# Expert outputs with w3 stationary on two column halves, and the mixing moved from VectorE to TensorE

## What is computed

```python
logits = x @ gate_w + gate_b
top_probs, top_idx = top_k(softmax(logits), 2)          # two experts of 16 for each token
dispatch = sum(one_hot(top_idx) * top_probs / sum(top_probs))
hidden = silu(x @ w1[e]) * (x @ w2[e])                  # for every expert e: 64 -> 128
expert_out = hidden @ w3[e]                             # 128 -> 64
out = h + sum_e expert_out[e] * dispatch[:, e]
```

## Time and profile before

| | us |
|---|---|
| median of 3 runs | 2246.7 |
| lowest and highest | 2244.17 and 2251.53 |
| profiled execution, own time | 2242.19 |
| its span | 2240.4 |

### The profile page before, as it was taken

One profiled execution on the slowest core, in us unless ns is written; L12 is line 12 of the kernel. 1 busy time (PEld: TensorE's weight loads), 2 busy tenths in 40 slices (PEclk: granted clock), 3 DMA queues, 4 the chain that ended last, 5 costly groups with the idle time before them and its releaser, 6 DMA issues.

```text
span 2240.4 us, 45957 instructions
## 1 busy us (share of the span) xinstructions
PE 2017.2 (90%) x15249; PEld 1837.6 (82%) x15249; DVE 1996.7 (89%) x6209; ACT 942.2 (42%) x2040; POOL 1454.0 (65%) x1657
## 2 busy tenths in 40 slices
PE   2468999989898999999899998989999998999899
PEld 1356789889798988889798897989888898988788
DVE  1257899999999999999999999999999999999998
ACT  1224443444444444444444444444444444433333
POOL 0388767578585858758575775858587685858700
PEclk9779999999999999999999999999999999998999
DMA  8787536466564646666463665746376674532200
GB/s 200 214 238 207 172 106 179 139 186 194 162 189 112 182 123 193 188 169 194 111 183 111 189 191 165 198 114 188 104 197 183 169 199 120 175 88 85 68 3 6
DMA packets 363145, 346.80 MB, mean 155 GB/s; under 512 B 49312, under 2 KB 313632, under 8 KB 362784
## 3 DMA queue, kind: packets, MB, share of 16 engines
q1 hardware_dynamic: 313760, 209.59, 34.8%
q0 software_dynamic: 49152, 134.28, 20.1%
HBM read 205.89 MB, written 137.89 MB: 153 GB/s over the span
## 4 chain that ended last, share of the span: by engine, by line
PE 60%; DVE 27%; issue 8%; POOL 2%; DMA 1%; ACT 1%; DVEq 0%; POOLq 0%; ACTq 0%
PE bank_o L637 15%; PE bank_h L628 10%; PE bank_h L629 9%; PE bank_d L693 9%; PE bank_d L703 7%; DVE ob L975 5%; DVE hid L964 4%; DVE wsam L1053 2%; DVE v_sb L1088 2%; PE bank_a L715 2%; PE bank_p L658 2%; POOL gath L574 2%; DVE v_sb L1081 2%; PE bank_p L657 1%; PE bank_p L663 1%
## 5 line engine op out<-in xcount | busy, mean ns | idle before, releaser
L574 POOL DMA_INDIRECT gath<-table,idx x1024 | 1127.0, 1101 | 271.4 <-issue 237.5
L637 PEld LDWEIGHTS bank_o<-w_sb,hid 128*128 128x128 f32 x4608 | 636.2, 199 | 75.4 <-issue 60.6
L637 PE MATMUL bank_o<-w_sb,hid 128*128 128x64 f32 x4608 | 630.8, 275 | 43.7 <-DVE ob L975 42.6
L628 PE MATMUL bank_h<-xsplit,w 128*128 128x384 f32 x1536 | 616.4, 401 | 28.3 <-DVE hid L964 27.7
L787 ACT ACTIVATE silu<-bank_h 128x384 f32<-128x384 f32 x768 | 380.6, 496 | 481.5 <-PE bank_h L629 476.5
L629 PE MATMUL bank_h<-xsplit,w 128*128 128x384 f32 x1536 | 532.0, 346 | 0.0
L975 DVE SCALAR_TENSOR_TENSOR ob<-bank_o,disp,ob 128x64 f32<-128x64 f32 x2160 | 474.5, 276 | 3.7 <-PE bank_o L637 3.4
L964 DVE TENSOR_TENSOR hid<-silu,bank_h 128x384 f32<-128x384 f32 x768 | 420.6, 548 | 25.1 <-ACT silu L787 18.2
L628 PEld LDWEIGHTS bank_h<-xsplit,w 128*128 128x128 f32 x1536 | 301.2, 196 | 59.4 <-DVE hid L964 35.2
L1053 DVE TENSOR_TENSOR wsam<-gath,cw 128x1024 f32<-128x1024 f32 x256 | 312.3, 1220 | 25.8 <-DMA gath<-table,idx 19.6
L693 PE MATMUL bank_d<-eye,wsam 128*128 128x128 f32 x2048 | 281.8, 283 | 30.1 <-DVE wsam L1053 26.6
(11 more groups left out here) (142 smaller groups left out, 1864.4 us busy)
## 6 DMA issues: line engine op xcount, KB each, us to landing
table<-pixmaj SPq DMA_DIRECT2D x80, 1024.0 KB, 10.0
xin<-x_dram SPq DMA_DIRECT2D x256, 256.0 KB
table<-pixmaj SPq DMA_DIRECT2D x32, 960.0 KB
table<-pixmaj SPq DMA_DIRECT2D x16, 1088.0 KB
gath<-table,idx POOLq DMA_INDIRECT x1024
out_dram<-ob SPq DMA_DIRECT2D x48, 96.0 KB
gath<-w_dram SPq DMA_DIRECT2D x4, 512.0 KB, 9.3
interp_sb<-interp_dram SPq DMA_DIRECT2D x1, 1024.0 KB, 5.5
```

Of the source, the lines that this page charges most:

```text
L574: pool.indirect_dma_start(out=gath[buf][:, p, :, :].rearrange("p a c -> p (a c)"), out_offset=None, in_=table[par], in_offset=bass.Indirec ...
L628: mm(bank[:, 0:GC], w12[:, e, which, 0, :], xsplit[gp][:], start=True, stop=False)
L637: last = mm(bank_o[n % 2][:, C * k:C * (k + 1)], hid[:, n % HB, 128 * k:128 * (k + 1)], w3_sb[:, e, :], start=True, stop=True)
```

## The change

W is done for a pair of experts q = 0 to 7 of a group, with w3 stationary (64 columns) and `hid` moving (384 columns): the first expert of the pair writes partitions 0 to 63 of the one bank `bank_o`, the second partitions 64 to 127. So the outputs have channels on the partitions and tokens on the columns, and the dispatch weight is no longer a scalar of the partition. The new steps:

- P9: PE transposes the dispatch weights of a group (3 transposes of 64 columns) into `bank_p`, ACT copies them to `dispT`. P8 gets two more small DVE instructions, which split the weights into a rounded and a remaining part.
- R, for each pair: one float32r matmul of 384 columns with the 128 x 128 matrix `sel` spreads the two weight rows of the pair over 64 partitions each, into `bank_p`; ACT copies them to `wide[q]`. R of pair q waits for the copy of q - 1, as there is one bank.
- W on DVE, for each pair: `scaled` = `bank_o` x `wide[q]` (384 columns, a ring of 5). W on PE waits for the product of the pair before.
- Z, for each half group: PE transposes 4 `scaled` blocks for each of 3 token blocks, accumulating in `bank_z` (12 transposes of 128 x 128).
- M2, for each half group: DVE adds both halves of `bank_z` to `ob` (2 instructions of 192 columns).
- O: SP stores the group (was M2). The setup gets three DVE instructions more and one small load.

X, its `hid` and all other steps are as before. The wait of `hid` for its ring slot is now for a pair. The second bank of `bank_o` became `bank_z`. All strings of `ORDER` are new. In the steady batches PE's order has between two R of the same group: D2 (4 times in a batch), X and W (3), W (2), X and Z (2), X, nothing at all, and other pairs of steps once each. Of the 21 such gaps one is empty, in the first group: `X R X R R W R D2 R X Z R X W R D2 R`.

```diff
-        bank_o = [ps(f"bank_o{i}") for i in range(2)]
+        bank_o, bank_z = ps("bank_o"), ps("bank_z")
...
                     elif kind == "W":
-                        g, e = args
-                        n = SLOTS * b + NE * g + e
-                        pe.wait_ge(hid_done, n + 1)
-                        wait(pe, eo_added, GT * (n - 1))
+                        g, q = args
+                        n = PAIRS * (NGRP * b + g) + q
+                        pe.wait_ge(hid_done, 2 * n + 2)
+                        wait(pe, eo_scaled, n)
+                        for h in range(2):
+                            last = mm(bank_o[C * h:C * (h + 1), 0:GC], w3_sb[:, 2 * q + h, :], hid[:, (2 * n + h) % HB, :],
+                                      start=True, stop=True)
+                        last.then_inc(eo_ready, 1)
+                    elif kind == "Z":
+                        g, half = args
+                        n = PAIRS * (NGRP * b + g) + HALF * half
+                        pe.wait_ge(eo_scaled, n + HALF)
+                        wait(pe, mix_v, 4 * (NGRP * b + g) + 2 * half)
                         for k in range(GT):
-                            last = mm(bank_o[n % 2][:, C * k:C * (k + 1)], hid[:, n % HB, 128 * k:128 * (k + 1)],
-                                      w3_sb[:, e, :], start=True, stop=True)
-                        last.then_inc(eo_ready, 1)
+                            for q in range(HALF):
+                                last = mm(bank_z[:, 128 * k:128 * (k + 1)], scaled[(n + q) % SB][:, 128 * k:128 * (k + 1)],
+                                          eye[:], start=q == 0, stop=q == HALF - 1, is_transpose=True)
+                        last.then_inc(mix_ready, 1)
+                    elif kind == "P9":
...
+                    elif kind == "R":
+                        g, q = args
+                        n = PAIRS * (NGRP * b + g) + q
+                        pe.wait_ge(dispT_stored, NGRP * b + g + 1)
+                        if q:
+                            pe.wait_ge(wide_stored, n)
+                        mm(bank_p[:, 0:GC], sel[:, 128 * q:128 * (q + 1)], dispT[:], start=True, stop=True).then_inc(wide_ready, 1)
...
+                        wait(act, eo_scaled, n - PAIRS + 1)
+                        copy(wide[:, q, :], bank_p[:, 0:GC]).then_inc(wide_stored, 1)
...
-                        for k in range(GT):
-                            if e:
-                                dve.wait_ge(eo_added, GT * (n - 1) + k + 1)
-                            stt(ob[gp][:, k, :], bank_o[n % 2][:, C * k:C * (k + 1)], disp[gp][:, k, e:e + 1],
-                                (ob[gp] if e else h2[g])[:, k, :], ALU.mult, ALU.add).then_inc(eo_added, 1)
...
+                    elif kind == "W":
+                        wait(dve, mix_ready, (n - SB) // HALF + 1)
+                        tt(scaled[n % SB][:], bank_o[:, 0:GC], wide[:, q, :], ALU.mult).then_inc(eo_scaled, 1)
+                    elif kind == "M2":
...
+                        both = bank_z[:, 0:GC].rearrange("p (k h c) -> p k h c", k=GT, h=2)
+                        link(mix, tt(ob[gp][:], both[:, :, 0, :], (ob[gp] if half else h2[g])[:], ALU.add))
+                        mix.inc(tt(ob[gp][:], both[:, :, 1, :], ob[gp][:], ALU.add))
...
+                        link(top, vcopy(dispr[:, :, 0, 0:NE], disp[:]))
+                        tt(dispr[:, :, 1, 0:NE], disp[:], dispr[:, :, 0, 0:NE].bitcast(F32),
+                           ALU.subtract).then_inc(disp_done, 1)
```

More of the change, by code:

```diff
@@ L58 @@
 HB = 4
+PAIRS = NE // 2
+HALF = PAIRS // 2
+SB = 5
 OFFSET_SCALE = 4.0
@@ L122 @@
     ("L", "sp"): [(i,) for i in range(8)],
-    ("M2", "sp"): [(i,) for i in range(3)],
+    ("M2", "dve"): [(i, j) for i in range(3) for j in range(2)],
+    ("O", "sp"): [(i,) for i in range(3)],
     ("P1", "dve"): [(i,) for i in range(3)],
@@ L143 @@
     ("P8", "dve"): [(i,) for i in range(3)],
+    ("P9", "pe"): [(i,) for i in range(3)],
+    ("P9", "act"): [(i,) for i in range(3)],
     ("Q", "sp"): [(i,) for i in range(4)],
+    ("R", "pe"): [(i, j) for i in range(3) for j in range(8)],
+    ("R", "act"): [(i, j) for i in range(3) for j in range(8)],
     ("S1", "act"): [(i,) for i in range(2)],
@@ L149 @@
     ("T", "sp"): [()],
-    ("W", "pe"): [(i, j) for i in range(3) for j in range(16)],
+    ("W", "pe"): [(i, j) for i in range(3) for j in range(8)],
+    ("W", "dve"): [(i, j) for i in range(3) for j in range(8)],
     ("X", "pe"): [(i, j) for i in range(3) for j in range(16)],
@@ L153 @@
     ("X", "dve"): [(i, j) for i in range(3) for j in range(16)],
-    ("Z", "dve"): [(i, j) for i in range(3) for j in range(16)],
+    ("Z", "pe"): [(i, j) for i in range(3) for j in range(2)],
 }
@@ L377, in build @@
         pick = sb("pick", [128, GT, NE])
-        disp = [sb(f"disp{i}", [128, GT, NE]) for i in range(2)]
+        disp = sb("disp", [128, GT, NE])
+        dispr = sb("dispr", [128, GT, 2, 2 * NE], F32R)
+        dispT = sb("dispT", [128, GC], F32R)
+        sel = sb("sel", [128, 128 * PAIRS], F32R)
+        wide = sb("wide", [128, PAIRS, GC])
+        scaled = [sb(f"scaled{i}", [128, GC]) for i in range(SB)]
         silu = [sb(f"silu{i}", [128, GC]) for i in range(2)]
@@ new lines, in run @@
+                        n = PAIRS * (NGRP * b + g) + q
[10 more added lines that the diff above has]
+                        wait(pe, mix_v, 4 * (NGRP * b + g) + 2 * half)
+                        for k in range(GT):
+                            for q in range(HALF):
[3 more added lines that the diff above has]
+                    elif kind == "P9":
+                        g = args[0]
+                        pe.wait_ge(disp_done, NGRP * b + g + 1)
+                        for k in range(GT):
+                            last = mm(bank_p[0:C, 128 * k:128 * (k + 1)],
+                                      dispr[:, k, :, :].rearrange("p a e -> p (a e)").bitcast(F32), eye[:],
+                                      start=True, stop=True, is_transpose=True)
+                        last.then_inc(dispT_ready, 1)
+                    elif kind == "R":
[5 more added lines that the diff above has]
+                        mm(bank_p[:, 0:GC], sel[:, 128 * q:128 * (q + 1)], dispT[:], start=True, stop=True).then_inc(wide_ready, 1)
@@ L808, in run @@
                         nc.scalar.activation(top_p[:, 1, :], top_p[:, 0, :], ACT.Tanh, scale=0.5).then_inc(gap_tanh, 1)
+                    elif kind == "P9":
+                        g = args[0]
+                        act.wait_ge(dispT_ready, NGRP * b + g + 1)
+                        wait(act, wide_ready, PAIRS * (NGRP * b + g))
+                        copy(dispT[0:C, :], bank_p[0:C, 0:GC]).then_inc(dispT_stored, 1)
+                    elif kind == "R":
+                        g, q = args
+                        n = PAIRS * (NGRP * b + g) + q
+                        act.wait_ge(wide_ready, n + 1)
+                        wait(act, eo_scaled, n - PAIRS + 1)
+                        copy(wide[:, q, :], bank_p[:, 0:GC]).then_inc(wide_stored, 1)
                     elif kind == "D2" and args[1] == 1:
@@ L1143, in _ @@
             run()
-PHASES_READY = 26
-SETUP_V = 32
+PHASES_READY = 29
+SETUP_V = 35
 OFF_N = 20
```

225 lines of the change are left out of this document (121 added, 104 removed), and 6 rows, old and new, of the table KINDS.

## The result

| | us |
|---|---|
| the changed kernel, median of 4 runs | 2229.5 (2227.6 to 2235.0) |
| the kernel before beside it | 2248.1 |
| ratio, 95% interval | 0.992 [0.990, 0.995] |
| profiled execution: own time, span, mean clock | 2235.0, 2233.2, 0.972 |

The change makes the kernel 0.8% faster. The forecast was 2.1% slower, so its sign was wrong. The kernel before had a mean granted clock of 0.954. Some executions fell in a slower state, up to 4940 us long; all ratios and mean clocks here are those of the others.

What follows compares the result with a forecast made beforehand. The prediction took PE's own stream as the bound, about 118.7 of 130.2 us a batch. Its terms summed to +3.0 us over 14.5 batches, +44, plus 2 at the end: 2293 us, 2.1% slower, range 2225 to 2355.

Steps and rivals of the forecast that it cites:

- The low clock, -1.0 us a batch: PE's time at half clock behind its waits for DVE: 1.0 us a batch given back, bounds 0 and 3.9.
- I am wrong if the low clock vanishes or grows: Sign of a wrong forecast: PE's low clock vanishing or growing; the other such sign was W far from 1.0 us.
- PE's stream, +5.0: PE's own work: 37.6 us a batch added by W, R and transposes against 32.6 removed; with W's bounds -4.1 to +20.3.
- W's 1.02: W of a pair on PE, halves side by side, mode switches included: 1.02 us, bounds 0.64 and 1.66.
- R's waits, +1.5: PE waiting at R for ACT's copy of the pair before: 1.5 us a batch, bounds 0.8 and 3.
- DVE's waits, -2.5: PE's waits for DVE, 5.1 us a batch: half, 2.5 us, given back by DVE's relief; bounds 0 and 5.1.
- its 13 us: ACT's new copies for R and P9: 13 us a batch, free at 42% busy, with any cost in PE's waits at R.
- The ends, +2: At the very end W, a product, Z and M2 stand where W and Z stood: +2 us once; setup additions covered.
- The sum: All terms of a batch together, +5.0 + 1.5 - 2.5 - 1.0: +3.0 us a batch.
- DVE was the true limit: Rival: all PE waits for DVE and all low clock go, -2.5 us a batch, about 2212 us; chance of faster 0.15.
- R becomes the chain: Rival: ACT's queue delays R's copy and PE stands behind each R, 2.5 to 3.5 us a batch more, 2330 to 2345 us; 0.12.
- the two of lost overlap: Rivals: W's halves on PE overlap by half, 2404 us, chance 0.06, or not at all, 2516 us, chance 0.04.

Runs made afterwards that it cites:

- Relieving DVE: The kernel before with one of Z's three additions left out in 15 of 16 experts, PE unchanged: ratios 0.980 and 0.979 to the kernel before; 2200.5 us.
- DVE loaded: The changed kernel with one more DVE reduction of 192 columns behind each product: 0.973 and 1.006 of the kernel before; 2262.4 us beside 2245.8.
- the extra matmuls: The kernel before with dummy float32 matmuls on PE, ten ahead of one W and four ahead of one X, in 12 batches: ratios 1.011, 1.014, 1.011.
- 16 us a batch of freed stream: The changed kernel with W in float32r, both experts of a pair accumulating in one bank without halves: 2191.4 us, 0.974 of the kernel before.

## Why the prediction was wrong

- **The low clock, -1.0 us a batch: the step that failed.** The prediction tied the low clock to PE's wait behind S3, took half of the waits as given back because the change "helps least where the waits are", and so gave back only a quarter of the clock. The place was right. But the 2.5 us that PE stood there in every batch became two pieces of 0.5 and 0.8, and the low clock fell from 85.0 to 27.2 us, 58 us in 11.2 batches; at half speed this is at most 2.6 us a batch. The prediction also took the wait as the only cause: widening the old W alone, at unchanged waits, took 44 us of low clock off. The new W moves 384 columns where the old one moved 64 behind each weight load. How the gain divides between wait and form stays open. And 2.6 is an upper bound: the wide W got 44 us of clock back, 22 by this count, and was 8 us faster. The forecast's "I am wrong if the low clock vanishes or grows" is nearly how it went.
- **PE's stream, +5.0: too large, by 1.2 or more.** W's 1.02 was right, Z and P9 step at 0.11 a transpose, R at 0.18 to 0.28 depending on what stands ahead of it. But the X behind them got cheaper: its first line takes 386 ns on the mean (`L650`, in the steady part) where `L628` took 402, and 96 of these are 1.5 us a batch; a part of it is the clock. Perhaps fewer X now stand directly behind W or Z with their weight load uncovered, which I had counted at every W both times; this was not measured. What is left of the batch when waits and clock are taken off is +3.8, and less where the clock is worth less than its bound.
- **R's waits, +1.5: measured 0.8.** 7.3 us in 11 waits and the 0.19 us that each hides. The gaps with X alone, at 0.15 each, cost nothing. With the stream, R is worth 4.4 a batch instead of 5.7.
- **DVE's waits, -2.5: measured -2.6 for W, X and P9, -3.4 with D2's.** The size is near, but partly by luck. The long wait behind S3, which was to stay in half, went nearly whole, and P9's wait for the last of P8, 0.8 us a batch, which had no term, came in its place.
- **W** came as forecast, and so did ACT: its 13 us a batch are hidden but for R's waits.
- **The ends, +2: measured about +8.** From the last start of the once-a-batch line to the end of the span it is 242.7 us (242.5 in two other traces of the changed kernel) where it was 234.2. This error goes the other way. From the first start of that line to the last the changed kernel is 17.5 us shorter, and the end takes half of it back, so that the profiled executions differ by 7 us only. The medians differ by 19, and there is one trace of the kernel before, so the figure is rough.
- **The sum** of a batch by these measures is +3.8 + 0.8 - 3.4 - 2.6 = -1.4, with -1.3 read. The four errors, 1.2 + 0.7 + 0.9 + 1.6, all have the same sign and together exceed the +3.0 that was forecast. That it comes out is no proof: the stream is what remains, so only R's, DVE's and the clock's terms are measured by themselves, and the clock's is a bound.
- **The rivals.** "DVE was the true limit" gave 2212 us and needed 6.5 us given back. DVE gave back 3.4 and the clock at most 2.6; the rest came from a cheaper stream. It named the right side of no change, and for a part by the right mechanism: the long wait for DVE and most of the low clock went together. But it kept the stream at +5.0 and knew nothing of W's form. "R becomes the chain" and the two of lost overlap did not happen.

## What to carry over

Follow the one wait at which the clock falls, not the load of the engine that is waited for. Relieving DVE left PE's wait at 2.0 us and the low clock where it was; a new order with DVE loaded had neither. Before you take half of a wait as given back, walk through the new order at that place, step by step. Ask as well what the engine runs around the wait: a matmul bound by its weight loads has free columns, and more columns in the same time kept the clock up here at unchanged waits.

Look in an experiment's own trace whether it did what it was for: the extra matmuls were in their place on these chips, but the wait wasn't. When a run is made shorter, the order around it must be made anew: 16 us a batch of freed stream gave 2.8 because the steps between two hand-overs had become too short to hide them.

## What the hardware showed unexpectedly

- Six float32 matmuls took 0.58 us with 128 moving columns and 0.59 with 64, and the kernel with the wider ones had the higher mean clock on three chips (+0.015, +0.012, +0.014), with the long wait of once a batch unchanged at 2.5 us on the one chip that was undisturbed.
- Two chains of float32 matmuls on the two column halves overlap in full: 0.80 us for four instructions of 384 columns, 1.43 on one half.
- The low clock came once a batch, at PE's longest wait: 12 stretches for 12 waits of over 1.5 us in the kernel before.
- The same kernel took 2246 us on two chips and 2481, 2484 and 2561 us on three others. There, ACT for instance stood for 6.5 us with nothing in the profile that it waited for:

```profile
1146.90 0.49 ACT L788 ACTIVATE silu<-bank_h 128x384 f32<-128x384 f32 x1 [1.90 <-PE bank_h L630]
1153.88 0.48 ACT L805 CAST xsplit<-bank_p 128x384 fp32r<-128x384 f32 x1 [6.50 <-remote]
```

  (the old kernel with DVE relieved). What it is was not found out. DVE's relief had the same ratio there (0.980 and 0.979), but the changed kernel with DVE loaded had 0.973 there and 1.006 on the other.
